# Decoder layer in float32 on one core: five of six cross units with one exponential for all heads, a new static order, and x parts on GpSimd

## What is computed

```python
# x: (32, 112, 256)   ctx: (32, 375, 256)
Q, K, V = (x @ W + b for W, b in ...)                      # 16 heads of 16
scores  = Q K^T * 16**-0.5 + slope_h * (key - query)       # self attention, ALiBi bias
x1      = layernorm(x + softmax(scores) V @ Wo + bo)
q = x1 @ xWq + xbq;  k = ctx @ xWk + xbk;  v = ctx @ xWv + xbv
sm      = softmax over the QUERIES of (q k^T / sqrt(16))   # cross attention: axis 1, not the keys
x2      = layernorm(x1 + (sm v) @ xWo + xbo)
# feed forward with simulated quantisation; act_qdq rounds to 16-bit integers by one maximum of the whole tensor
g  = act_qdq(act_qdq(x2) @ w_gate.T);  s = 16-bit sigmoid(g);  u = act_qdq(act_qdq(x2) @ w_up.T)
h  = act_qdq(act_qdq(g * s) * u)
out = layernorm(x2 + h @ w_down.T)
```

## Time and profile before

| | |
|---|---|
| median of 3 runs | 1305.83 us (1305.64 to 1305.86) |
| the profiled execution | 1304.4 us |
| its span, first to last instruction | 1302.6 us |
| mean granted PE clock over the span | 0.959 |
| attention pass, first x transposed to last x2 | 38.8 to 985.3 us |
| up stage | about 1060 to 1145 us |

### The profile page before, as it was taken

One profiled execution on the slowest core, in us unless ns is written; L12 is line 12 of the kernel. 1 busy time (PEld: TensorE's weight loads), 2 busy tenths in 40 slices (PEclk: granted clock), 3 DMA queues, 4 the chain that ended last, 5 costly groups with the idle time before them and its releaser, 6 DMA issues. The chain is left out here.

```text
span 1302.6 us, 28828 instructions
## 1 busy us (share of the span) xinstructions
PE 1140.7 (88%) x8466; PEld 833.1 (64%) x8466; DVE 1001.3 (77%) x2239; ACT 1068.6 (82%) x4083; POOL 345.5 (27%) x431
## 2 busy tenths in 40 slices
PE   1689999999999999999999999999866987778598
PEld 1466666666666666666666666666535976667598
DVE  6268888888888878888788878888853559967688
ACT  1368999998999989999899989999863579968695
POOL 0223334333334333334433333433210000000044
PEclk9899999999999989999999999999976999989799
DMA  5100000100000100000000000010000000000033
GB/s 159 35 16 17 21 20 21 37 21 20 19 20 20 32 26 19 20 19 20 27 29 22 19 20 19 20 30 26 5 7 5 1 1 1 0 1 1 25 102 99
DMA packets 35111, 33.26 MB, mean 26 GB/s; under 512 B 4164, under 2 KB 34748, under 8 KB 35004
## 3 DMA queue, kind: packets, MB, share of 16 engines
q1 hardware_dynamic: 32704, 31.50, 7.9%
q10 hardware_dynamic: 2300, 0.66, 0.3%
HBM read 24.81 MB, written 7.34 MB: 25 GB/s over the span
## 5 line engine op out<-in xcount | busy, mean ns | idle before, releaser
L582 ACT ACTIVATE Px<-score,nmax_h 125x112 f32<-125x112 f32 x1024 | 349.5, 395 | 4.2 <-DVE nmax_h L783 3.1
L582 ACT ACTIVATION_READ_ACCUMULATOR Px<-score,nmax_h 125x1 f32 x1024 | 247.8, 249 | 0.0
L571 ACT ACTIVATE Ps<-score,nmax_s 112x112 f32<-112x112 f32 x512 | 177.1, 435 | 6.0 <-DVE nmax_s L790 6.0
L571 ACT ACTIVATION_READ_ACCUMULATOR Ps<-score,nmax_s 112x1 f32 x512 | 147.7, 289 | 0.0
L783 DVE TENSOR_REDUCE nmax_h<-score 125x8 f32<-125x896 f32 x128 | 138.5, 1082 | 7.2 <-PE score L1028 6.3
L502 POOL TENSOR_TENSOR Qbd_hi<-Qx_hi,mask 128x448 fp32r<-128x448 f32 x64 | 59.7, 933 | 293.8 <-DVE Qx_lo L799 293.8
L1028 PE MATMUL score<-Qbd_hi,KxT_hi 64*125 64x448 f32 x384 | 91.6, 472 | 35.9 <-POOL Qbd_lo L502 26.6
L523 POOL TENSOR_TENSOR rstd<-vare,half 112x1 f32<-112x1 f32 x64 | 35.1, 548 | 320.9 <-DVE vare L875 320.9
L1120 PE MATMUL outX<-Px,Vn 125*32 125x224 f32 x1536 | 109.4, 373 | 5.0 <-DVE Vn L766 5.0
L623 ACT ACTIVATE PsT<-work 112x448 f32<-112x448 f32 x128 | 74.6, 583 | 33.1 <-PE work L1155 32.4
L1608 PE MATMUL gbank<-xq_hi,w_upT_hi 128*128 128x448 f32 x192 | 73.8, 385 | 27.8 <-ACT xq_lo L1402 27.8
(11 more groups left out here) (244 smaller groups left out, 3500.0 us busy)
## 6 DMA issues: line engine op xcount, KB each, us to landing
ctx_in<-in_ctx SPq DMA_DIRECT2D x32, 375.0 KB
x_in<-in_x SPq DMA_DIRECT2D x32, 112.0 KB, 2.1
x_scratch<-x SPq DMA_DIRECT2D x32, 112.0 KB, 1.9
x2T_all<-x_scratch SPq DMA_DIRECT2D x32, 112.0 KB, 2.1
out<-x2T_all SPq DMA_DIRECT2D x32, 112.0 KB, 1.9
raw_w_up<-in_w_up SPq DMA_DIRECT2D x1, 768.0 KB, 5.8
raw_w_down<-in_w_down SPq DMA_DIRECT2D x1, 768.0 KB, 7.4
raw_w_gate<-in_w_gate SPq DMA_DIRECT2D x1, 768.0 KB, 9.5
```

What stands on the lines that cost most here:

```text
L571: ins = act.activation(Ps[:, g, :], score[slot][0:L, h // QUAD, (h % QUAD) * L:(h % QUAD + 1) * L], ACT.Exp, bias=nmax_s[:, g:g + 1], accu ...
L582: ins = act.activation(Px[u % 2][:, h, :], score[SLOT_OF[f"C{u}"]][0:C, h // QUAD, (h % QUAD) * L:(h % QUAD + 1) * L], ACT.Exp, bias=maxim ...
```

## The change

- `BY_HEAD` is now `(5,)`: units 0 to 4 of the cross attention are shifted, unit 5 stays by head.
- The lists of all engines in `step` and both tables of PSUM uses are written anew. The operations of a batch are the same apart from those that units 1, 3 and 4 need: five `copy_max`, `exp_shifted`, `sum_cross`, `transpose_max` and `shift` in place of two.
- In the up pass the parts of x for groups 1 to 7 are made by POOL (`up_parts`), with a semaphore of their own; group 0 and the other passes stay on ACT.

The diff, cut to its core:

```diff
-BY_HEAD = (1, 3, 4, 5)
+BY_HEAD = (5,)
 ...
 WORK_USES = (
-    (("Qx", 2), ("AVs0", 3), ("PT2", 3), ("ctxT0", 3), ("ctxT1", 3), ("V0", 3), ("V1", 3), ("Vs", 4), ("x2T", 0), ("PT0", 4),
-     ("V2", 3), ("x1T", 3)),
-    (("K1", 2), ("Qs", 4), ("PT3", 3), ("AVs1", 3), ("Os", 3), ("K0", 3), ("PT1", 4), ("Ox", 1), ("xT", 5), ("Ks", 5)),
+    (("K0", 3), ("Os", 3), ("Ox", 1), ("Vs", 4), ("xT", 5), ("PT1", 4), ("Ks", 5), ("V2", 3), ("K1", 3), ("AVs0", 4),
+     ("PT2", 4), ("ctxT1", 4)),
+    (("x2T", 0), ("V0", 3), ("PT0", 4), ("V1", 3), ("x1T", 3), ("Qx", 3), ("Qs", 5), ("ctxT0", 4), ("PT3", 4), ("AVs1", 4)),
 )
 SLOT_USES = (
-    (("C5", 1), ("C1", 2), ("C2", 2), ("C4", 2)),
-    (("C0", 2), ("S0", 4), ("C3", 2), ("S1", 4)),
+    (("C2", 2), ("C4", 2), ("C5", 2), ("C1", 3)),
+    (("C3", 2), ("S1", 4), ("C0", 3), ("S0", 5)),
 )
 ...
             def step(n0, n1, n2, n3, n4, n5, n6):    # SP
-                if n4:
-                    load_ctx(n4)
+                if n6:
+                    load_x(n6)
+                if n5:
+                    load_ctx(n5)
                 if n1:
                     save_x2(n1)
-                if n6:
-                    load_x(n6)
 ...
         @block.gpsimd
         def _(pool):
             pool.memset(ones[:], 1.0).then_inc(ones_done, 1)
 
+            def up_parts(g, p):
+
+                pool.wait_ge(product, g * 2 + (NH - 2))
+                pool.tensor_copy(xh[p][0][:], xpart(x2T_all, g, 0))
+                pool.tensor_copy(xh[p][1][:], xpart(x2T_all, g, 1)).then_inc(up_parts_done, 1)
+
+            def up_step(g, p, last):
+                if not last:
+                    up_parts(g + 1, 1 - p)
+
+            over_groups(pool, up_step)
 ...
                 if last:
                     parts(HIDDEN, 0, 0)
-                else:
-                    parts(UP, g + 1, 1 - p)
                 sigmoid(g, 1)
 ...
-                pe.wait_ge(x_parts, g + (stage * NG + 1))
+                if stage == UP and not (isinstance(g, int) and g == 0):
+                    pe.wait_ge(up_parts_done, g)
+                else:
+                    pe.wait_ge(x_parts, g + {GATE: 1, UP: NG + 1, HIDDEN: NG + 2}[stage])
```

More of the change, by code:

```diff
@@ L724, in step @@
                     exp_self(n4, 1)
+                if n5:
+                    hi_queries_self(n5)
+                if n3:
+                    hi_keys_cross(n3, 1)
+                if n2:
+                    exp_by_head(n2, 5)
+                if n4:
+                    even_self(n4, 0)
+                if n3:
+                    copy_max(n3, 0)
+                if n4:
+                    hi_context(n4, 0)
+                if n3:
+                    exp_shifted(n3, 0)
+                if n4:
+                    copy_probs(n4, 2)
+                    copy_probs(n4, 3)
+                if n2:
+                    even_cross(n2)
+                if n3:
+                    copy_max(n3, 1)
+                if n4:
+                    hi_context(n4, 1)
+                    even_self(n4, 1)
+                if n3:
+                    exp_shifted(n3, 1)
+                if n4:
+                    hi_keys_cross(n4, 0)
+                if n1:
+                    copy_x2T(n1)
+                if n5:
+                    exp_self(n5, 0)
+                if n3:
+                    copy_max(n3, 2)
             iterations(act, step)
@@ L937, in step @@
                     pick_self(n4, 1)
+                if n2:
+                    pick_cross(n2)
+                if n4:
                     divide_self(n4, 1)
+                if n3:
+                    reciprocal_cross(n3, 0)
                 if n5:
                     max_self(n5, 0)
+                if n3:
+                    normalise_values(n3, 0)
+                if n4:
+                    lo_keys_cross(n4, 0)
+                if n1:
+                    largest(n1)
+                if n3:
+                    max_cross(n3, 2)
+                if n4:
+                    residual(n4, 0)
+                if n3:
+                    sum_cross(n3, 1)
+                if n4:
+                    moments(n4, 0)
+                if n2:
+                    residual(n2, 1)
                 if n4:
@@ L1236, in step @@
                 if n2:
+                    shift(n2, 4)
                     cross_values(n2, 2)
@@ L1239, in step @@
                     self_scores(n4, 1)
[L1240 to L1241 removed]
+                if n3:
+                    project_T(n3, "Qx", w["xWq"], x1T, "x1T")
+                    values_cross(n3, 2)
+                if n2:
+                    cross_scores(n2, 5)
+                if n5:
+                    project_T(n5, "Qs", w["aWq"], xT, "xT")
+                if n3:
+                    keys_cross(n3, 1)
+                if n2:
+                    cross_values(n2, 3)
+                if n3:
+                    cross_scores(n3, 0)
+                if n4:
+                    self_values(n4, 0)
+                if n2:
+                    cross_values(n2, 4)
+                if n4:
+                    transpose_ctx(n4, 0)
+                if n3:
+                    transpose_max(n3, 0)
+                    cross_scores(n3, 1)
+                    shift(n3, 0)
+                if n4:
+                    transpose_probs(n4, 2)
+                    transpose_probs(n4, 3)
+                if n2:
+                    cross_values(n2, 5)
+                if n4:
+                    transpose_ctx(n4, 1)
+                if n3:
+                    transpose_max(n3, 1)
+                if n4:
+                    self_values(n4, 1)
+                if n3:
+                    shift(n3, 1)
+                if n5:
+                    self_scores(n5, 0)
             iterations(pe, step)
```

244 lines of the change are left out of this document (89 added, 155 removed).

## The result

The changed kernel takes **1431.78 us** (median of four runs, 1430.22 to 1432.68) against 1305.74 us: ratio 1.097, 95% interval [1.095, 1.099]. It is 126 us slower, where 1317 us was forecast in a range of 1291 to 1342. "Slower" was right, the size and the reason were not: the way came out right by luck, as the last sections show.

The account below looks back on a forecast made before the run. PE, 94.9% busy in the attention pass, was taken as the bound, at 28.8 us a batch after the change. 1304.4 + 19 (attention) - 8 (up stage) = 1315.4, plus 1.4 to the median: 1317 us, range 1291 to 1342.

Parts of the forecast that it names:

- Moves on the queues: SP and POOL in the attention pass: same three DMAs and ten POOL operations a batch, POOL busy 35%, costed at nothing.
- The rule: POOL shares SBUF interfaces with DVE and contends with two-SBUF-input DVE instructions; weighed against the up stage, full gain kept.
- Batch 28.2 us, Qbd wait 0.96 us that goes: Attention pass: a batch cost 28.2 us before; PE's 0.96 us wait for Qbd_lo would be gone or nearly so.
- ACT -4.4 us a batch, no bound: Attention pass: shifting three units saves ACT 4.4 us a batch, to some 21 of 28, so it stops bounding.
- PE +1.5 us: Attention pass: transposes and shifts add 1.71 us a batch, 0.20 comes back from new neighbours; net +1.5 us.
- DVE +3.2 us, from 23.1 to 26.3: Attention pass: three more sums of 1.07 us a batch make DVE the second fullest engine, over 90%.
- Rival 3: Attention pass: DVE sets the pace, PE waiting for nmax_c or Vn; 1344 to 1360 us, chance 0.15.
- Waits 0.55 us: Attention pass: PE's remaining waits in the new order, taken as 0.55 us a batch between ends 0 and 1.43.
- +19: Attention pass: 31 steps at 0.6 us more each, from first x transposed to last x2, 19 us slower.
- Rival 2: Attention pass: PE has hidden room and ACT was the bound; batch 27.7 us, total 1282 us, chance 0.09.
- Up stage -8 us: Up stage: x parts moved to POOL, DVE becomes the bound at 8.8 us a group, 8 us gained.
- the fourth rival: Up stage: parts on POOL give nothing, copies and DVE slowing each other or products waiting; 1325 us, chance 0.08.

Follow-up runs that it names:

- pause_before_qbd1: The changed kernel with one added wait: POOL waits before Qbd 1 until the batch's fifth Vn is done; 1303.04 us, ratio 0.997.
- burst_behind_vn: The changed kernel with POOL's step cut in two, six block-diagonal products and x1b issued only after the batch's last Vn; 1288.49 us, ratio 0.986.
- split_and_glu_wait: burst_behind_vn plus one wait: up-stage pairs of casts on POOL, from the second on, wait for DVE's glu product; 1284.39 us, ratio 0.983.
- split_short_sums: split_and_glu_wait with DVE's sums over the exponentials reading 2 of 112 columns, only its time being of use; 1284.22 us.
- bias_in_the_middle: The changed kernel with POOL's sums xb and x1b issued between the products Kbd 0 and Qbd 1; 1358.76 us, ratio 1.041.

## Why the prediction was wrong

**The step that failed** is "Moves on the queues", where POOL's ten operations were "the same", "busy 35%", and costed at nothing because "the cover is most of a 28 us step". The amount was the same and POOL was never late for anyone. The kernel before had two rows without a pause a batch, of 6.7 us (it starts in the earlier trace rows) and of 3.1 us, with at most two products next to each other. The change joined their work to one row of 9.1 us, in which six products follow each other directly, and put a `Vn` beside the second of the six. The price is 32.97 - 28.45 = 4.5 us a batch by `pause_before_qbd1`, against the 4.2 us between 28.8 forecast and 33.0 measured; times 28 batches that is 127 us, and the run took 129 off. Against `burst_behind_vn`, which has no steady hold on DVE in the attention pass, it is 143 us. The sum forecast 1317 and missed by 115, since other terms of it were too high, as told below.

**The rule was at hand and was asked about the wrong place.** It was weighed against the up stage alone, and dismissed for the attention pass by POOL's durations (0.93 to 0.98 us). But the one that waits is DVE, so DVE's durations were the rows to read, and they said so in the kernel before (DVE, then POOL, in the timeline of the kernel before):

```profile
631.49 0.58 DVE L766 TENSOR_TENSOR Vn<-Vx,rZc 125x128 f32<-125x128 f32 x1
```

```profile
631.17 0.74 POOL L529 TENSOR_TENSOR xb<-x_in,abo 112x256 f32<-112x256 f32 x1
631.87 0.98 POOL L502 TENSOR_TENSOR Kbd_hi<-Ks_hi,mask 128x448 fp32r<-128x448 f32 x1
```

This `Vn` took 0.58 us in place of 0.28, and it ended 0.20 us after POOL had passed from `xb` to `Kbd_hi`. The normalised x1 behind it took 0.90 us where it takes 0.40 in the changed kernel. The mean of the group, 368 ns against a usual 280, was a second sign. The Trainium skill, SBUF — State Buffer, section "SBUF: two separate sides", says that the port pair of VectorE and GpSimd is an exclusive lock: the one that starts first keeps it for the whole instruction. The traces agree for one instruction, in both directions (`Vn` behind `xb`, the second cast behind glu). By that rule the long `Vn` would have cost one product's rest, 0.6 us; the trace shows that the holder can keep it over its next instructions too: 4.3 us through five, 7.9 us through nine. Nor does the one that starts first always win: in `burst_behind_vn` the product at 567.52 is shown to start 0.76 us before the `Vn` and is the one drawn out.

**The terms of the sum**, read in the run without holds on DVE in the loop (`split_and_glu_wait`), where they can be seen:

- *Batch 28.2 us, Qbd wait 0.96 us that goes*: right; the wait for Qbd_lo is gone in the changed kernel already.
- *ACT -4.4 us a batch, no bound*: right, 76% busy without holds.
- *PE +1.5 us*: too high by 1.0. The transposes give way after 0.20 us as priced, and scores before a shift after 0.71; the shift itself gives way after 0.29 us, not the 0.37 shown in the earlier trace rows, so 3 x 0.49 - 0.20 = 1.3 us. PE's busy time rose by 0.5 only, from 26.8 to 27.3 us a batch; the clock went from 0.98 to 1.00 with it.
- *DVE +3.2 us, from 23.1 to 26.3*: the three sums are right in size (1.08 us each), and shown hidden by `split_short_sums`. DVE comes to 24.4 us a batch and not to 26.3: the 23.1 of the kernel before had about 1.3 us of holds in it (`Vn`, x1, x2), which are gone here. Rival 3 named "PE waiting for DVE's nmax_c or Vn" as its sign. The sign came, but not by DVE's amount of work: rival 3's mechanism is refuted.
- *Waits 0.55 us*: 9.2 of 564 us, 0.45 a batch. The hold-free batch is 27.7 us, not 28.8: with the last x2 at 975.04 us against 984.85 the attention part is worth -9.8 us where +19 was forecast. Its sign was wrong; the total came out slower only by what was costed at nothing. Of the 1.1 us too much, 0.2 is PE's work and 0.1 the waits, up to 0.5 is the clock that rose by 2%; the rest is open.
- *Rival 2's numbers* (27.7 us, 1282) were met by the repaired kernel, but not its reason: PE is full there, 98%, and not hidden.
- *Up stage -8 us*: 5.6 to 5.9. The missing part is the glu product held by 0.65 us in a group, the fourth rival, given 0.08; it was true in part. With the hold away the group takes 8.78 us, the forecast's 8.8, and the stage 8.5 us less than before.

The clock is a consequence with a price of its own, which no run takes apart from the wait: at half clock behind each 3.4 us wait PE does its blocks slower for 6 us, and every run that took the wait away had 0.98 to 1.00 back.

## What to carry to other kernels

When a change makes a row of POOL instructions longer or moves it, list which DVE instructions stand beside it, and look in the trace of before for such DVE instructions that last longer than their fellows (a group's mean above its usual duration is a sign). A busy share of 25% on POOL says nothing about what a row without a pause does to DVE, and a held instruction is counted as busy. The repair is a wait on POOL for the DVE instruction that must get in, or the row moved; then look again at both sides, since in `burst_behind_vn` a `Vn` still stood beside the row and POOL's product was drawn out in its place, while PE stayed busy 98% of the stretch.

## What the runs showed of the hardware that was not expected

- A DVE product, copy or scaling beside a row of POOL instructions that are ready waits for more than one of them: 4.3 us through five, 7.9 us through nine, with no bound found. The ones held here were `Vn` (two inputs), rZrep and the normalised x1 and x2 (one input each) and the glu product; sums, maxima and operations that read PSUM beside the same rows kept their times (`KxT_lo` 0.60 us at 405.41, the reductions 1.08).
- Memsets on POOL, which read nothing, hold DVE's copy as well: 1.15 us where it takes 0.22 to 0.33. The Trainium skill, SBUF — State Buffer, section "SBUF: two separate sides", makes reading a condition only for DVE operations with two SBUF inputs, and the copy has one; the trace agrees as far as it goes.
- The hold can go the other way: in `burst_behind_vn` a product of POOL's row that is shown to start 0.76 us before a `Vn` took 1.84 us in place of 0.93, and the `Vn` its usual 0.28.
- DVE gets in as soon as POOL has nothing ready (0.74 us in `pause_before_qbd1`). In a row without a pause it sometimes gets in earlier, at a boundary that I can't predict: behind `xb` with two products to come in the loop of the kernel before, one instruction later for the same pair in its unrolled last batches (at 801.36 us a `Vn` of 1.46 us), behind `x1b` with four to come in `bias_in_the_middle`, ahead of `xb` and `x1b` in the changed kernel, and only for the last one in the rows of extra products. Which boundary gives way stays open.
- Blocked waits cost PE twice: 3.4 us of idle time, then a granted clock of 0.50 until some 6 us after the work went on.
